# Causal attentions of a hybrid network, by pairs of heads

## What is computed

```python
q = (x @ Wq).reshape(b, t, h, d) * scale      # h = 16 heads, d = 8
k = (x @ Wk).reshape(b, t, h, d) * scale
v = (x @ Wv).reshape(b, t, h, d)
dot = jnp.einsum('bqhd,bkhd->bhqk', q, k)
dot = jnp.where(causal[None, None], dot, -jnp.inf)
attn = jax.nn.softmax(dot, axis=-1)
out = jnp.einsum('bhqk,bkhd->bqhd', attn, v).reshape(b, t, h * d)
return out @ Wo
```

## Time and profile before

| what | value |
|---|---|
| time, median of 3 runs | 4997.43 us (4973.68 to 5001.73) |
| profiled execution, its time | 4969.21 us |
| profiled execution, its span | 4967.5 us |
| PE busy | 4473.0 us (90%) |
| DVE busy | 2379.6 us (48%) |
| ACT busy | 1719.1 us (35%) |
| POOL busy | 843.7 us (17%) |
| mean granted TensorE clock | 0.912 of full speed |

### The profile page before, as it was taken

How to read it: one execution, slowest core, us unless ns; L and a number is a source line. 1 busy time by engine, 2 the same in 40 slices (tenths; PEclk the granted TensorE clock), 3 DMA queues, 4 the chain that set the end, 5 groups by cost and what they waited for, 6 DMA issues and landing times.

```text
span 4967.5 us, 76834 instructions
## 1 busy us (share of the span) xinstructions
PE 4473.0 (90%) x30219; PEld 2776.4 (56%) x30275; DVE 2379.6 (48%) x6906; ACT 1719.1 (35%) x3496; POOL 843.7 (17%) x1441
## 2 busy tenths in 40 slices
PE   7998989889898898988989889899898998989989
PEld 3556645565455654556545575455754457545575
DVE  3435634356443554435544355444554445544455
ACT  2322432325333343333433234333343333433334
POOL 2003110031100311103011040111401114011130
PEclk8989979999899998999989999899998999998989
DMA  2000000000000000000000000000000000000000
GB/s 68 1 1 1 1 6 1 1 1 1 6 1 1 1 1 6 1 1 1 1 6 1 1 1 1 6 1 1 2 1 6 1 1 2 1 3 1 1 1 3
DMA packets 19571, 17.25 MB, mean 3 GB/s; under 512 B 2462, under 2 KB 18799, under 8 KB 19183
## 3 DMA queue, kind: packets, MB, share of 16 engines
q1 hardware_dynamic: 19183, 11.99, 0.8%
HBM read 9.89 MB, written 2.10 MB: 2 GB/s over the span
## 4 chain that ended last, share of the span: by engine, by line
PE 80%; DVE 6%; POOL 6%; ACT 5%; issue 3%; DVEq 0%; ACTq 0%; POOLq 0%; SPq 0%
PE banks L984 7%; PE banks L974 7%; PE banks L988 7%; PE banks L880 7%; PE banks L908 6%; PE banks L825 6%; PE banks L920 3%; POOL work L478 3%; PE banks L865 3%; PE banks L1180 3%; PE banks L1201 2%; PE banks L1167 2%; PE banks L1074 2%; PE banks L1047 2%; PE banks L1023 2%
## 5 line engine op out<-in xcount | busy, mean ns | idle before, releaser
L1369 DVE CUSTOM_DVE_ANT_0 work<-banks,mask_row 128x512 f32<-128x512 f32 (+3 forms) x1024 | 451.6, 488 | 274.0 <-PE banks L880 270.6
L880 PE MATMUL banks<-work 32*128 32x512 f32 (+3 forms) x2048 | 526.7, 493 | 11.4 <-DVE work L1369 11.4
L908 PE MATMUL banks<-work 32*128 32x256 f32 (+3 forms) x2048 | 512.7, 504 | 20.8 <-ACT work L638 20.8
L638 ACT ACTIVATE work<-banks 128x384 f32<-128x384 f32 (+1 forms) x768 | 368.9, 526 | 441.9 <-PE banks L908 440.3
L437 POOL TENSOR_TENSOR rstd<-rstd,half 128x2 f32<-128x2 f32 x128 | 87.5, 703 | 2451.2 <-DVE moments L1297 1834.2
L654 ACT ACTIVATE work<-banks 128x512 f32<-128x512 f32 (+1 forms) x384 | 228.8, 596 | 687.6 <-PE banks L984 687.4
L1441 DVE TENSOR_TENSOR work<-work,banks 128x512 f32<-128x512 f32 (+1 forms) x384 | 263.5, 686 | 344.8 <-PE banks L988 344.5
L984 PE MATMUL banks<-xnT,wg 128*128 128x512 f32 (+1 forms) x768 | 417.8, 627 | 0.0
L988 PE MATMUL banks<-xnT,wu 128*128 128x512 f32 (+1 forms) x768 | 406.1, 611 | 0.0
L447 POOL TENSOR_SCALAR_AFFINE_SELECT work<-work 128x128 f32<-128x128 f32 (+1 forms) x768 | 252.6, 332 | 897.4 <-ACT work L638 886.1
L974 PEld LDWEIGHTS banks<-wd,work 128*128 128x128 f32 (+1 forms) x3072 | 360.6, 191 | 57.3 <-issue 57.3
(11 more groups left out here) (255 smaller groups left out, 7254.4 us busy)
## 6 DMA issues: line engine op xcount, KB each, us to landing
x_next<-in_L_attn_a_x_dram SPq DMA_DIRECT2D x8, 256.0 KB, 2.8
out_dram<-x SPq DMA_DIRECT2D x8, 256.0 KB, 2.2
wg<-in_L_ffn_Wg_dram SPq DMA_DIRECT2D x1, 1376.0 KB
wu<-in_L_ffn_Wu_dram SPq DMA_DIRECT2D x1, 1376.0 KB
wd<-in_L_ffn_Wd_dram SPq DMA_DIRECT2D x2, 512.0 KB
wk_l<-in_L_attn_a_Wk_dram SPq DMA_DIRECT2D x1, 512.0 KB, 7.8
wv_l<-in_L_attn_a_Wv_dram SPq DMA_DIRECT2D x1, 512.0 KB, 6.5
wq_l<-in_L_attn_a_Wq_dram SPq DMA_DIRECT2D x1, 512.0 KB, 7.2
```

The source lines that it names most:

```text
L638: eng.activation(prob4[:, G % 2, hh, C_AT[j]:C_AT[j] + C_N[j]], bank(3 + c % 3)[:, 0:C_N[j]], ACT.Exp).then_inc(s_exp, 1)
L880: m = eng.matmul(bank(k % 3)[:, col:col + N], q4[own, G, P * t:P * t + P], k4[own, G, 0:N], start=True, stop=True)
L908: m = eng.matmul(bank(3 + c % 3)[:, col:col + N], k4[own, G, P * s:P * s + P], q4[own, G, P * s:T], start=True, stop=True)
L1369: m = eng.tensor_tensor_reduce(out=summed[:, k % 2, col:col + N], in0=bank(k % 3)[:, col:col + N], in1=mask_row[:, T - N:T], scale=1.0, sc ...
```

## The change

Jobs are ordered by pairs of heads. A pair `p` has six row jobs and six column jobs (`PAIR` = 6): two heads at 512, two at 384, two at the last size. `pair_job` gives the pair, its group, the head and the size for job `k`. An attention has eight pairs.

- Columns are `LEAD` = 8 jobs behind rows, 16 before. The turned head goes; the head of a column job is that of its pair.
- `max_columns` and `shift_q` run for each pair: four transposes again, after the second step of the next pair but before the third, whose column job is the first that needs them; the subtraction works on the pair's 64 partitions. `max_tile` has four slots instead of two, and its memset at the start of a turn doubles.
- Projections run two in a row, three row jobs after each of two such pairs of projections; the row jobs left follow all projections.
- Values: keys 0 and 1 in one piece after column job 1 of the next group, keys 2 and 3 after its job 3 as before. `group_rows` is after job 7 of the next group, ACT's `group_columns` after 5 (6 before).
- The last eight column jobs, which have no row jobs beside them, rotate over banks 0, 1, 2, 4, 5, 3, 0, 1, with waits to match.

```diff
-LEAD = 16
+ROW_TILES = [[3], [2], [1, 0]]
+NPAIR = H // 2
+PAIR = 6
+LEAD = PAIR + 2
...
-        max_tile, at4 = part(at4, [2, NT, G4 * 32])
+        max_tile, at4 = part(at4, [4, NT, G4 * 32])
...
-        def column_head(c):
-
-            return (c + 2) % G4
+        def pair_job(k):
+
+            p, r = k // PAIR, k % 2
+            return p, p // 2, 2 * (p % 2) + r, k % PAIR // 2
+
+        def pair_rows(p):
+            return slice(64 * (p % 2), 64 * (p % 2) + 64)
+
+
+        COL_BANK = [3 + c % 3 for c in range(JOBS4 - LEAD)] + [0, 1, 2, 4, 5, 3, 0, 1]
...
-                if G >= 1 and c % ROWS4 == 6:
+                if G >= 1 and c % ROWS4 == 5:
                     group_columns(eng, n, G - 1, 6 + (G - 1) % 2)
...
-            def max_columns(G):
-                eng.wait_ge(s_max, JOBS4 * n + ROWS4 * (G + 1))
-                if G == 0:
+            def max_columns(p):
+                G = p // 2
+                eng.wait_ge(s_max, JOBS4 * n + PAIR * (p + 1))
+                if p == 0:
                     eng.wait_ge(p_st, 2 * NG * (n + 1))
-                if G >= 2:
+                if G >= 2 and p % 2 == 0:
                     eng.wait_ge(a_o, NG * n + G - 1)
                 for t in range(NT):
-                    m = eng.transpose(bank(6 + G % 2)[:, P * t:P * t + P],
-                                      max_tile[:, G % 2, t, :], ident[:, :])
+                    m = eng.transpose(bank(6 + G % 2)[:, P * t:P * t + P], max_tile[:, p % 4, t, :], ident[:, :])
                 m.then_inc(s_maxT, 1)
 
             def score_columns(c):
-                G, hh = c // ROWS4, column_head(c)
-                if c % ROWS4 == 0:
-                    eng.wait_ge(s_shift, NG * n + G + 1)
-                if c >= 3:
+                p, G, hh, j = pair_job(c)
+                if c % PAIR == 0:
+                    eng.wait_ge(s_shift, NPAIR * n + p + 1)
+                if c >= JOBS4 - LEAD:
+                    tail = c - (JOBS4 - LEAD)
+                    if tail < 3:
+                        eng.wait_ge(s_max, JOBS4 * n + JOBS4 - 2 + tail)
+                    else:
+                        eng.wait_ge(s_exp, JOBS4 * n + c - 5)
+                elif c >= 3:
                     eng.wait_ge(s_exp, JOBS4 * n + c - 2)
...
-                eng.wait_ge(s_keep, JOBS4 * n + ROWS4 * G + G4 * (last + 1))
+                eng.wait_ge(s_keep, JOBS4 * n + ROWS4 * G + PAIR + 2 * (last + 1))
...
-            for k in range(3):
-                score_rows(k)
-            for i in range(2, 2 * NG):
+            for i in range(2, 2 * NG, 2):
                 project(i)
-                score_rows(i + 1)
-            for k in range(2 * NG + 1, JOBS4 + LEAD):
+                project(i + 1)
+                if i < 2 * NG - 2:
+                    for k in range(3 * i // 2 - 3, 3 * i // 2):
+                        score_rows(k)
+            for k in range(PAIR, JOBS4 + LEAD):
                 if k < JOBS4:
                     score_rows(k)
                 if k >= LEAD:
                     c = k - LEAD
                     G, at = c // ROWS4, c % ROWS4
                     score_columns(c)
-                    if at == 7:
-                        weigh_group(G, [0])
-                    if at == 11:
-                        weigh_group(G, [1])
+                    if G >= 1 and at == 1:
+                        weigh_group(G - 1, [0, 1])
                     if G >= 1 and at == 3:
                         weigh_group(G - 1, [2, 3])
-                    if G >= 1 and at == 9:
+                    if G >= 1 and at == 7:
                         group_rows(eng, n, G - 1, 6 + (G - 1) % 2)
-                if k % ROWS4 == 2 and ROWS4 <= k < JOBS4 + 3:
-                    max_columns(k // ROWS4 - 1)
+                if k % PAIR == 1 and PAIR < k < JOBS4 + PAIR:
+                    max_columns(k // PAIR - 1)
+            weigh_group(NG - 1, [0, 1])
             weigh_group(NG - 1, [2, 3])
...
-                def shift_q(G):
-                    eng.wait_ge(s_maxT, NG * n + G + 1)
-                    eng.tensor_tensor(q4[:, G, :], q4[:, G, :], bank(6 + G % 2), ALU.subtract)\
-                       .then_inc(s_shift, 1)
-
-                for k in range(JOBS4 + 3):
+                def shift_q(p):
+                    G = p // 2
+                    eng.wait_ge(s_maxT, NPAIR * n + p + 1)
+                    q = q4[pair_rows(p), G, :]
+                    eng.tensor_tensor(q, q, bank(6 + G % 2)[pair_rows(p), :], ALU.subtract).then_inc(s_shift, 1)
+
+                for k in range(JOBS4 + 1):
                     if k < JOBS4:
                         row_max(k)
+                    if k % PAIR == 0 and k > 0:
+                        shift_q(k // PAIR - 1)
                     for G in range(2):
-                        if k == ROWS4 * (G + 1) + LEAD + 9:
+                        if k == ROWS4 * (G + 1) + 9 + LEAD:
                             heads_out(n, G, 6 + G, rden4)
-                    if k % ROWS4 == 2 and k >= ROWS4:
-                        shift_q(k // ROWS4 - 1)
```

More of the change, by code:

```diff
@@ L423, in _, with col_bank @@
             turn(B - 1, True)
-        def column_head(c):
-            return (c + 2) % G4
+        def pair_job(k):
[4 more added lines that the diff above has]
+        COL_BANK = [3 + c % 3 for c in range(JOBS4 - LEAD)] + [0, 1, 2, 4, 5, 3, 0, 1]
+        def col_bank(c):
+            return COL_BANK[c]
         def pad_bank(i):
@@ L441, in pool_attn @@
             for c in range(JOBS4):
-                G, hh, j = c // ROWS4, column_head(c), c % ROWS4 // G4
+                p, G, hh, j = pair_job(c)
                 eng.wait_ge(s_exp, JOBS4 * n + c + 1)
@@ L637, in act_attn @@
                 eng.wait_ge(s_col, JOBS4 * n + c + 1)
-                eng.activation(prob4[:, G % 2, hh, C_AT[j]:C_AT[j] + C_N[j]], bank(3 + c % 3)[:, 0:C_N[j]],
+                eng.activation(prob4[:, G % 2, hh, C_AT[j]:C_AT[j] + C_N[j]], bank(col_bank(c))[:, 0:C_N[j]],
                                ACT.Exp).then_inc(s_exp, 1)
-                if G >= 1 and c % ROWS4 == 6:
+                if G >= 1 and c % ROWS4 == 5:
                     group_columns(eng, n, G - 1, 6 + (G - 1) % 2)
@@ L852, in stacked @@
             return st[64 * r:64 * r + KROWS, h // 2, cols]
-        def row_tiles(k):
-            return ([3], [2], [1, 0])[k % ROWS4 // G4], k % G4
         def pe_attn(eng, n, w):
@@ L869, in score_rows @@
             def score_rows(k):
-                G = k // ROWS4
-                tiles, hh = row_tiles(k)
+                p, G, hh, j = pair_job(k)
                 if k % ROWS4 == 0:
@@ L877, in score_rows @@
                 col = 0
-                for t in tiles:
+                for t in ROW_TILES[j]:
                     N = (t + 1) * P
@@ L905, in score_columns @@
                 col = 0
-                for s in C_JOBS[c % ROWS4 // G4]:
+                for s in C_JOBS[j]:
                     N = T - P * s
-                    m = eng.matmul(bank(3 + c % 3)[:, col:col + N], k4[own, G, P * s:P * s + P],
+                    m = eng.matmul(bank(col_bank(c))[:, col:col + N], k4[own, G, P * s:P * s + P],
                                    q4[own, G, P * s:T], start=True, stop=True)
@@ L1358, in row_max @@
                 def row_max(k):
-                    G = k // ROWS4
-                    tiles, hh = row_tiles(k)
+                    p, G, hh, j = pair_job(k)
                     eng.wait_ge(s_row, JOBS4 * n + k + 1)
-                    if G >= 2:
-                        eng.wait_ge(s_maxT, NG * n + G - 1)
+                    if p >= 4 and k % PAIR == 0:
+                        eng.wait_ge(s_maxT, NPAIR * n + p - 3)
                     if k >= 2:
```

3 lines of the change are left out of this document (2 added, 1 removed).

## The result

The changed kernel takes 5057.8 us (median of 4 runs, 5051.4 to 5065.9), the kernel before 4986.2 (4 runs, 4973.7 to 5001.7): ratio 1.0143 [1.0103, 1.0182]. It is slower, by 72 us or 1.4%. The profiled executions differ by 82: the span was 4967.5 us and is 5049.6.

A forecast was written before the change was run, and what follows sets the result against it. TensorE bounds the kernel, its cost set by strips, breaks, and round trips to DVE and ACT. Attentions at the high clock +35 us and clock +80 gave +115 on the 4997 median: 5112 us, range 5040 to 5190 (50%); overall 4940 to 5190.

The forecast's parts named there:

- Head: Start of an attention up to its first column job: 16.8 us where it took 22.96, a gain of 6.1 us.
- Duo in one strip: Steps 0,1 of a pair, row and column job in the same strip: 2.7 us behind a break, where it took 1.07.
- rival d: Nothing is held up behind a strip, steps 0,1 take 1.7 us: kernel 4995 us, down to 4965; 18%.
- rival b: Matmuls start strictly in program order, steps 0,1 cost 3.1 us: kernel 5157 us; 4%.
- Handover: Transposes of the maxima to step 2's column job, which waits for DVE's subtraction: 0.84 us exposed on PE, eight times an attention.
- The six banks, and the values in two pieces: Last column jobs: bank wait goes, ACT is late next; 0.7 us until values may start, then 1.75+0.8 and 4.55 us.
- An attention at the high clock: Whole causal attention: +8.3 us behind the first column job, with the head +2.2 us; 16 times, +35 us.
- Rival e: DVE's way back is covered and nothing is held up, so the head's 6.1 us stay whole: 4900 us; 12%.
- turning point: Slower once steps 0,1 and handovers lose over 6.1 us an attention more than the later steps' overlap gains.
- Clock: Sparse work lets the clock fall: 12 us more at 1.2 GHz per attention (bounds 0 and 30), 16x5.0=+80 us.
- Rival c: Waits as worked out but the clock falls no oftener: 5032 us, down to 5010; 16%.

The follow-up runs named there:

- The exchange of the two jobs, rows first: Changed kernel with both row jobs of steps 0 and 1 of a pair issued ahead of both column jobs: ratio 0.9924 to the kernel before, 4940.8 us.
- the cover: Changed kernel with values of key 0 or group_rows put right behind the transposes, while DVE subtracts: ratio 0.9893 to the kernel before, 4939.8 us.
- the combined kernel: Changed kernel with row jobs ahead of column jobs in steps 0 and 1, and values or group_rows behind the transposes: ratio 0.9748 to before, 4860.9 us.
- new head alone: Kernel before with only projections two in a row and three row jobs behind each of two such pairs; lead stays 16: ratio 0.9975, 4955.5 us.
- same-strip kernel: Kernel before with column jobs in plain head order, so row and column job of each step share a strip: ratio 1.1338, 5636.9 us.

## Why the prediction was right, and what was too large

The direction and the range held. The forecast was 5112 us and the time is 5058: 11 of the 54 us are the median of the kernel before, 4986 over four runs for the 4997 that I started from; 33 are in the sum, +115 where the spans show +82; the last 10 are that the profiled execution of before stood 17 us under its median and that of after 6.

- *Head:* 16.8 predicted, 16.6 measured, and 15.7 in the attention shown with its clock at 0.90. The gain is the 6.1 us of the working, to 0.3; over all 16 attentions it is 6.6 on average.
- *Duo in one strip:* 2.7 predicted, 2.67 measured, with the second row job 0.96 us late. A whole group, from its transposes at 2730.77 to those at 2745.68 of the same trace, takes 14.91 us, 14.95 predicted. The exchange of the two jobs shows its cause; rival d (nothing held up) is refuted, and so is rival b, by which the second row job would have come 1.4 us in.
- *Handover:* the column job 1.4 us behind the transposes, 1.44 measured, the subtraction on 64 partitions 0.69. So 0.86 us is exposed, 0.84 predicted. That it was real time is shown by the useless matmul, which fits into it without making anything later, and by the cover, 3.5 us an attention behind the head.
- *The six banks, and the values in two pieces:* the end without bank waits was worked out as part of 59.0 us behind the first column job; measured 59.2. The six banks themselves brought 0.1 us.
- *An attention at the high clock:* +2.2 us predicted and measured, +35 us over 16. Rival e is refuted with this; its turning point was the right one, since everything behind the head costs 8.5 us more (59.2 for 50.7) and the head gains 6.4; the combined kernel has 6.7 of the 8.5 back, and with it the head's gain stays.
- *Clock:* the mechanism was right and its size was off. The price holds: rows with columns at 0.84 took 7.5 us more for 17 us at the low level, 0.44 a us, against the 0.42 worked out. The number doesn't: 12 us more per attention at the low clock were taken from bounds of 0 and 30. The span shows 85 us more of it, some 5 an attention, and by length the clock costs 49 us more and not 80. This is the mis-sized term: 12 predicted, 4.8 measured in an attention (302 for 226 us in 16). The reason is in the records of the clock. Ten of the 16 attentions had falls before, which began in the last 3 us of the head, among the paced row jobs or right behind them, like the one of the earlier trace rows. The change took those row jobs away, and no fall begins there any more; it put new ones into 15 attentions at the handovers; the rows with columns went from 73 to 184 us at the low level, while the heads lost 25 and the stretches behind lost 11. I had only added. The run with the new head alone agrees: it keeps paced row jobs, and its falls begin there.
- Rival c (waits as worked out, no more falls) would have been 5032. The time lies between it and the forecast, 26 us from the one and 54 from the other, and about half way when both start from the 4986 of the four runs. The direction does not hang on the clock; the size does. The useless matmuls show that the falls behind the heads are worth 100 us in after, but 47 of the like were there before.
- *What a page said:* that transposes do not count as busy time for the clock in the same way (the Trainium skill, TensorE: Matmul & The Clock Gate, Part 4: PE-mode transpose). The falls behind handovers, although four transposes stand in each, agree with it, and so does it that a plain matmul beside them stopped the falls; no run compares equal amounts of both. The strict order of starts that the Trainium skill states (same page, Part 3: Packing small matmuls, The mechanism) is contradicted once more: in the run with rows first both row jobs of a duo start together (2681.49 and 2681.50), the second ahead of the first one's second pass (2682.02), and in after the second row job starts at 2737.53, ahead of three passes of the column job before it in the program (2737.74 to 2738.07).

## What to carry to other kernels

When jobs share the array by row strips, count what each strip has queued, not what the engine is busy with: a job behind another of the same strip also holds up the jobs of free strips behind it, and two exchanged jobs were worth 2%. Put work that must be done anyway, here on the whole array, behind the instruction whose answer is awaited. And price a sparse stretch twice, once for its length and once for the clock that it lets fall, by looking at where the falls were before the change and whether those places stay.

## What the hardware showed beyond that

- A PE that is busy without a gap can still lose its clock: in after, the rows with columns have PE busy for 52.89 of 52.89 us and the clock at 0.84, in the same-strip kernel for 58.45 of 58.70 at 0.58. There the columns alone then lay at 0.50, 27.5 us at 95% busy, where the same jobs held 1.00 in the earlier trace rows. In another attention of the kernel before, these jobs lost the high level themselves (windows of PE alone, in its columns alone and tail). So neither the busy share nor the kind of job alone tells the level; what does is left open.

```profile
717.50:720.80 3.30, 2.57 (x20) 1.00 0.01 2
720.80:734.50 13.70, 13.13 (x76) 0.50 0.00 1
```

- One float32 matmul of 256 columns per handover, whose result is thrown away, left no attention with a fall behind its head and made the kernel 2% faster; six of the same in an attention, four of them between overlapping jobs, made the kernel before 1.3% slower.
- Where the clock falls repeats in the changed kernel from the second attention on (81.1 and 83.1 us in two executions), and an edit worth 0.1 us an attention moved the time by some 30. It does not repeat as well in every program: the kernel before took 4957 to 5017 us in one set, with mean clocks of 0.915 to 0.899.
